# Attention in pairs of steps: one reciprocal a pair, its scaled copy on ScalarE, values and residual one unit later

## The chip, the cores and the metric

The kernel runs on one core of a Trainium2 chip. A core has TensorE (matrix products), VectorE, ScalarE, GpSimd, and SyncE, which here only issues transfers. The engines run side by side and wait for each other through semaphores. The metric is the device time of one execution in microseconds.

## The reference, cut to what matters

Two layers of attention and feed-forward over x of 2 x 256 x 512 with a context of 2 x 512 x 512. The change touches only the softmax attention of the second layer, with 32 query heads, 8 key and value heads and a head width of 128:

```
q, k = rmsnorm(x_norm @ Wq.T), rmsnorm(ctx @ Wk.T)      # 8 key heads serve 4 query heads each
v = ctx @ Wv.T
scores = einsum('bhqd,bhkd->bhqk', q, k) / sqrt(128) + mask
attn   = softmax(scores, axis=-1)
out    = einsum('bhqk,bhkd->bhqd', attn, v)
x      = x + out @ Wo.T
```

After it comes a gated low-rank layer and the store of x.

## The kernel before, in words

All products keep float32 accuracy by splitting each operand into a high half (float16) and a low half (the float16 of what is left): `three_products` (lines 263 to 267) issues three matmuls of 128x128 by 128x512 in place of one.

A **step** is one query head on one tile of 128 tokens against the 512 context positions of its batch: k = 16 g + j, with g one of 8 key heads and j from 0 to 15. Four steps (the four query heads of a key head) on one token tile are a **unit**; there are 32 units and 128 steps. A step goes through the engines like this:

- TensorE: `scores` (line 571), three matmuls into one of four PSUM banks.
- VectorE: `masked_scores` (L1385) adds the mask from SBUF and keeps the row's minimum of the negated scores in `mneg`, writing to one of four slots of `f32r`.
- ScalarE: `exponentials` (L905), with the row sum into `psum_col`.
- VectorE: `inverse_sum` (L1390), the reciprocal of one column, into `rinv[:, 0]`.
- GpSimd: `prob_hi`, first the same reciprocal times 16384 into `rinv[:, 1]` (L1102), then the high half of the probabilities into one of four slots of `hlr` (L1103).
- VectorE: `prob_lo` (L1396), the low half into the same slot, from `f32r`, `rinv[:, 1]` and the high half. It reads two tensors of SBUF.
- SyncE: `prob_transpose` (L353), one DMA transpose of both halves from `hlr` to the unit's buffer `pT[m]`, m the unit's number within g.
- TensorE, per unit: `values` (line 585), 4 x 3 matmuls from `pT` and `v_sb` into bank 4 + m. ScalarE writes the high half of the output (`o_hi`, L910), TensorE subtracts it in the bank (`residual`, L602, one matmul), and ScalarE writes the rest (`o_lo`, L914).

The order on each engine is written out by hand in loops over g, the first of them unrolled. VectorE per step j: scores of j, reciprocal of j - 1, low half of j - 2. TensorE per step: scores of step j (four ahead of VectorE by the banks), at the third step of a unit the residual of the unit before, and a quarter of the values of the unit three back. ScalarE: the exponential, then `o_hi` at the first and `o_lo` at the fourth step of a unit. GpSimd waits for the reciprocal and for the transpose that freed its slot of `hlr` (four steps back). SyncE waits for the low half. After the loops TensorE has the values of the last units and the output projection (`o_group`), a row of products with nothing else among them.

The key lines of VectorE's loop:

```
masked_scores(j, k, m % QT_PER_B, first)
inverse_sum((j - 1) % 4, k - 1)
prob_lo((j - 2) % 4, k - 2, ...)
```

Of the kernel before, what the change touches and what calls it, by code (L numbers as in the profile page):

```python
# [57 lines left out]
def xattn_ffn_kernel(nc, x_rows, ctx_nat, first_chunks, ctx_t, mask, params, wkv, moe, moe_b3, wq, wo, a_w, b_w, l_wq, l_keys, out):  # L58
    gates_dram = nc.dram_tensor("gates_dram", (NE, TOK), F32, kind="Internal").ap()
    with ExitStack() as ctx:  # L60
# [39 lines left out]
        cq = xT[:, :, :, :].rearrange("p a b c -> p (a b c)")  # L100
        xqT = pT1[:, 0:2, :, :].rearrange("p a b (k t) -> p (a b) k t", k=KC)
        ones128 = pT1[:, 2, 0, 0:P]
        pT2 = sb("pT2", [P, 4, 2, GW], F16)
# [122 lines left out]
        s_e = sem("s_e")  # L226
        s_r0 = sem("s_r0")
        s_ph = sem("s_ph")
        s_pl = sem("s_pl")
# [45 lines left out]
        def _(sp):  # L275
# [71 lines left out]

            def prob_transpose(j, split):

                slot = j % 4  # L350
                sp.wait_ge(s_nl, 16 + NT * KVH)
                sp.wait_ge(s_pl, split)
                sp.dma_start_transpose(pT[j // REP][:, slot, :, :].rearrange("p l (c q) -> p (l c) q", c=SC),  # L353
                                       hlr[:, slot, :, :].rearrange("p l x -> p (l x)")).then_inc(s_pT[slot], 16)

            for j in range(4 * REP):
                prob_transpose(j, j + 1)
            with sp.Fori(1, KVH) as g:
                for j in range(4 * REP):
                    prob_transpose(j, sp.to_reg(16 * g + j + 1))  # L360
            for n in range(3, KVH):
# [12 lines left out]
        def _(pe):  # L374
# [209 lines left out]

            def values(w, gw, mw, c, wait_bank=True):

                if c == 0:
                    for h in range(REP):
                        pe.wait_ge(s_pT[h], 16 * (w + 1))
                    if wait_bank:  # L590
                        pe.wait_ge(s_ol, w + 1)
# [12 lines left out]

            def attention(g, first):
                for j in range(4 * REP):
                    k = 16 * g + j
# [29 lines left out]
            for j in range(4):  # L637
                scores(0, j, j, True)
            attention(0, True)
            for h in range(4):  # L640
                pe.wait_ge(s_qT[h], 16 * KVH)
            with pe.Fori(1, KVH) as g:
                attention(g, False)
# [5 lines left out]
            residual(4 * KVH - 2, 2)  # L649
            for c in range(SC):  # L650
                values(4 * KVH - 1, KVH - 1, 3, c)

# [75 lines left out]
        def _(act):  # L728
# [187 lines left out]
            def attention(g, first):  # L916
                for j in range(4 * REP):
                    k = 16 * g + j
                    m, hh = divmod(j, REP)
                    if not first or j >= 3:  # L920
                        exponentials(j, k)
# [7 lines left out]
            for j in range(3):  # L929
                exponentials(j, j)  # L930
            attention(0, True)
            with act.Fori(1, KVH) as g:
                attention(g, False)
            for m in range(2):
                o_hi(4 * KVH - 4 + m, m)
# [76 lines left out]
        def _(pool):  # L1012
# [80 lines left out]

            def prob_hi(j, k, first):
                summed, freed = k + 1, 4 * (k - j)
                if not first:
# [6 lines left out]
                pool.tensor_scalar(hlr[:, j % 4, 0, :], f32r[:, j % 4, :], rinv[:, 0, j % 4:j % 4 + 1], PSCALE,  # L1103
                                   ALU.mult, ALU.mult).then_inc(s_ph, 1)

            for j in range(4):
                prob_hi(j, j, True)
            with pool.Fori(1, 4 * KVH) as u:
                for j in range(4):
                    prob_hi(j, 4 * u + j, False)  # L1110

# [17 lines left out]
        def _(dve):  # L1129
# [257 lines left out]

            def inverse_sum(j, k):
                dve.wait_ge(s_e, k + 1)
                dve.reciprocal(rinv[:, 0, j % 4:j % 4 + 1], psum_col[:, j % 4:j % 4 + 1]).then_inc(s_r0, 1)  # L1390

            def prob_lo(j, k, earlier=None):
# [3 lines left out]
                dve.scalar_tensor_tensor(out=hlr[:, j % 4, 1, :], in0=f32r[:, j % 4, :], scalar=rinv[:, 1, j % 4:j % 4 + 1],  # L1396
                                         in1=hlr[:, j % 4, 0, :], op0=ALU.mult, op1=ALU.subtract).then_inc(s_pl, 1)

            def attention(g, first):
                for j in range(4 * REP):  # L1400
                    k = 16 * g + j
                    m, hh = divmod(j, REP)
                    masked_scores(j, k, m % QT_PER_B, first)
                    if not first or j >= 1:
                        inverse_sum((j - 1) % 4, k - 1)
                    if not first or j >= 2:
                        prob_lo((j - 2) % 4, k - 2, None if first and j < 6 else 4 * g + (j - 2) // REP)

# [3 lines left out]
            end = 16 * KVH  # L1412
            inverse_sum(3, end - 1)
            prob_lo(2, end - 2, 4 * KVH - 1)
            prob_lo(3, end - 1, 4 * KVH - 1)

# [128 lines left out]
```

## Time and profile before

| what | value |
|---|---|
| time, median of 3 runs | 695.01 us (694.28 to 697.63) |
| the profiled execution | 695.37 us, its span 693.2 us |
| busy over the span | TensorE 91%, VectorE 63%, GpSimd 59%, ScalarE 49% |
| attention stage | from about 376 to 574 us |
| after it | output projection on TensorE, to about 640 us, then the last layer |

Times in the rows are microseconds from the start of the span. Busy shares are averages over stages with different limits, so the stage of the change has to be read alone. A wait is put down to the semaphore that came last. PE is TensorE, PEld its weight loads, DVE VectorE, ACT ScalarE, POOL GpSimd, SPq the queue of SyncE.

### The profile page before, as it was taken

What the parts mean: (1) busy time and instruction counts of PE and PEld (TensorE: products, weight loads), DVE (VectorE), ACT (ScalarE), POOL (GpSimd) and SP (SyncE); (2) the same over time, 40 slices, a digit from 0 to 9 for tenths busy, and PEclk for the clock granted to TensorE, in tenths of its full rate; (3) what the DMA queues carried; (4) which work ended last, traced back from release to release, by engine and by line L of the source; (5) the groups of instructions that cost most, each with busy time, mean ns of one, the idle gap of its engine ahead of it and who ended that gap; (6) DMA issues with size and microseconds to landing.
All of it is one profiled execution on the core that took longest, in us unless ns stands there. A gap on an engine that the chain in (4) does not pass through costs nothing.

```text
span 693.2 us, 11377 instructions
## 1 busy us (share of the span) xinstructions
PE 627.6 (91%) x3004; PEld 280.2 (40%) x3004; DVE 438.5 (63%) x1055; ACT 340.1 (49%) x690; POOL 409.8 (59%) x438
## 2 busy tenths in 40 slices
PE   5729989889999999999998779999999999999997
PEld 2314534334444444444443234444444444444453
DVE  5999897253444334755555989999999990000673
ACT  4514544233433332566667566667777663233132
POOL 4923134254455543178787878889898892548111
PEclk9958999899999999999999999999999999999999
DMA  8802034444444432179878999999999995325001
GB/s 327 356 0 76 10 76 99 93 140 148 137 122 136 143 105 96 52 179 180 208 165 221 180 160 172 175 179 175 174 176 174 175 175 106 101 81 183 0 1 61
DMA packets 200312, 95.62 MB, mean 138 GB/s; under 512 B 187962, under 2 KB 188090, under 8 KB 197341
## 3 DMA queue, kind: packets, MB, share of 16 engines
q1 hardware_dynamic: 197490, 90.49, 54.6%
q10 hardware_dynamic: 2795, 4.79, 2.2%
q8 instruction: 14, 0.23, 0.1%
q14 instruction: 13, 0.11, 0.0%
HBM read 48.03 MB, written 1.09 MB: 71 GB/s over the span
## 4 chain that ended last, share of the span: by engine, by line
PE 41%; DVE 19%; issue 16%; POOL 15%; DMA 4%; SPq 2%; ACT 2%; DVEq 1%; POOLq 1%; ACTq 0%
PE ps L265 13%; PE ps L267 13%; PE ps L266 13%; POOL hlr L1103 8%; POOL hlr L1023 4%; POOL wsp L1023 3%; DVE f32r L1385 3%; DVE st L1146 1%; DVE nw L1158 1%; DVE nw L1157 1%; DVE f32r L1162 1%; DMA wsp<-hlr 1%; DMA stage<-in_first_chunks 1%; DVE xT L1221 1%; SPq L314 1%
## 5 line engine op out<-in xcount | busy, mean ns | idle before, releaser
L1023 POOL TENSOR_TENSOR wsp<-stage,wsp 128x512 f16<-128x512 f32 (+1 forms) x93 | 134.5, 1469 | 136.2 <-ACT wsp L761 73.7
L905 ACT ACTIVATE f32r<-f32r,mneg 128x512 f32<-128x512 f32 x128 | 92.4, 722 | 61.1 <-DVE mneg L1385 59.8
L1023 POOL TENSOR_TENSOR hlr<-f32r,hlr 128x512 f16<-128x512 f32 x52 | 60.6, 1173 | 88.3 <-ACT hlr L814 55.0
L1103 POOL TENSOR_SCALAR hlr<-f32r,rinv 128x512 f16<-128x512 f32 x128 | 106.1, 829 | 0.0
L1396 DVE SCALAR_TENSOR_TENSOR hlr<-f32r,rinv,hlr 128x512 f16<-128x512 f32 x128 | 96.0, 750 | 13.0 <-POOL hlr L1103 8.7
L1385 DVE CUSTOM_DVE_ANT_0 f32r<-ps,nmask 128x512 f32<-128x512 f32 x128 | 87.5, 684 | 0.9 <-issue 0.6
L1102 POOL TENSOR_SCALAR rinv<-rinv 128x1 f32<-128x1 f32 x128 | 68.1, 532 | 23.3 <-DVE rinv L1390 11.7
L1354 DVE SCALAR_TENSOR_TENSOR f32r<-ps,par,f32r 128x512 f32<-128x512 f32 x18 | 13.5, 751 | 73.3 <-PE ps L267 60.9
L1304 DVE TENSOR_REDUCE ss<-f32r 128x4 f32<-128x512 f32 x48 | 32.9, 685 | 42.4 <-ACT f32r L802 42.3
L265 PE MATMUL ps<-q_sb 128*128 128x512 f16 x128 | 49.3, 385 | 10.1 <-POOL q_sb L1023 7.3
L265 PE MATMUL ps<-xT,wsp 128*128 128x512 f16 x144 | 55.9, 388 | 2.7 <-DVE stage L1346 2.7
L267 PE MATMUL ps<-xT,wsp 128*128 128x512 f16 x144 | 56.0, 389 | 0.0
L266 PE MATMUL ps<-xT,wsp 128*128 128x512 f16 x144 | 55.9, 389 | 0.0
L265 PE MATMUL ps<-k_sb,q_sb 128*128 (+1 forms) x128 | 49.0, 383 | 7.6 <-DVE mneg L1385 6.2
L265 PE MATMUL ps<-wsp,xT 128*128 128x512 f16 x128 | 48.6, 379 | 2.9 <-POOL wsp L1023 2.8
L802 ACT ACTIVATE f32r<-ps 128x512 f32<-128x512 f32 x48 | 28.6, 597 | 45.1 <-PE ps L267 45.1
L266 PE MATMUL ps<-q_sb 128*128 128x512 f16 x128 | 49.3, 385 | 0.0
L267 PE MATMUL ps<-q_sb 128*128 128x512 f16 x128 | 49.3, 385 | 0.0
L266 PE MATMUL ps<-k_sb,q_sb 128*128 (+1 forms) x128 | 48.8, 381 | 0.0
L267 PE MATMUL ps<-k_sb,q_sb 128*128 (+1 forms) x128 | 48.8, 381 | 0.0
L267 PE MATMUL ps<-wsp,xT 128*128 128x512 f16 x128 | 48.5, 379 | 0.0
L266 PE MATMUL ps<-wsp,xT 128*128 128x512 f16 x128 | 48.5, 379 | 0.0
(229 smaller groups left out, 1298.1 us busy)
## 6 DMA issues: line engine op xcount, KB each, us to landing
stage<-in_moe SPq DMA_DIRECT2D x18, 512.0 KB, 3.8
stage<-in_wq SPq DMA_DIRECT2D x8, 1024.0 KB, 5.2
stage<-in_wo SPq DMA_DIRECT2D x8, 1024.0 KB, 4.8
stage<-in_moe SPq DMA_DIRECT2D x18, 256.0 KB, 3.3
hlr<-gates_dram ACTq DMA_DIRECT2D x18, 256.0 KB, 3.2
k_sb<-in_wkv SPq DMA_DIRECT2D x3, 1024.0 KB, 18.8
stage<-in_first_chunks SPq DMA_DIRECT2D x4, 512.0 KB, 5.8
q_sb<-in_ctx_nat SPq DMA_DIRECT2D x1, 2048.0 KB, 14.9
```

Source lines behind the costliest of these rows:

```text
L265: pe.matmul(dst, lhs[0], rhs[1], start=start, stop=False, skip_group_check=True)
L266: pe.matmul(dst, lhs[1], rhs[0], start=False, stop=False, skip_group_check=True)
L267: return pe.matmul(dst, lhs[0], rhs[0], start=False, stop=stop, skip_group_check=True)
L802: act.activation(f32r[:, j % 2, :], ps[j % 4][:, :], ACT.Square).then_inc(s_sq, 1)
L905: act.activation(f32r[:, j % 4, :], f32r[:, j % 4, :], ACT.Exp, bias=mneg[:, j % 4:j % 4 + 1], scale=-1.0, accum_out=psum_col[:, j % 4:j % ...
L1023: return pool.tensor_tensor(dst_lo, src, dst_hi, ALU.subtract)
L1102: pool.tensor_scalar(rinv[:, 1, j % 4:j % 4 + 1], rinv[:, 0, j % 4:j % 4 + 1], PSCALE, None, ALU.mult)
L1103: pool.tensor_scalar(hlr[:, j % 4, 0, :], f32r[:, j % 4, :], rinv[:, 0, j % 4:j % 4 + 1], PSCALE, ALU.mult, ALU.mult).then_inc(s_ph, 1)
L1304: dve.tensor_reduce(ss[:, j % 2, :], f32r[:, j % 2, :].rearrange("p (h d) -> p h d", h=REP), AX_X, ALU.add).then_inc(s_ss, 1)
L1354: dve.scalar_tensor_tensor(out=tile, in0=bank[:, :], scalar=mb[:, 1, bass.ds(e, 1)], in1=tile, op0=ALU.add, op1=ALU.mult).then_inc(s_hx, 1)
L1385: dve.tensor_tensor_reduce(f32r[:, j % 4, :], ps[j % 4][:, :], nmask[:, qt, :], 0.125, BIG, ALU.add, ALU.min, mneg[:, j % 4:j % 4 + 1]).th ...
L1396: dve.scalar_tensor_tensor(out=hlr[:, j % 4, 1, :], in0=f32r[:, j % 4, :], scalar=rinv[:, 1, j % 4:j % 4 + 1], in1=hlr[:, j % 4, 0, :], op ...
```

## The change: what it does

- VectorE works in pairs of steps. Per pair p: two low halves (of pair p - 2), one reciprocal of two columns (of pair p - 1), two scores (of pair p).
- The scaled copy of the reciprocals (L1102) leaves GpSimd and becomes one ScalarE instruction per pair (`scaled_inverses`), with a new semaphore s_sc that the low halves wait for.
- GpSimd's high half waits for the reciprocal of its pair.
- TensorE computes the values of the unit four back (before: three) and the residual of the unit five back (before: four). After the loop there are three units of values where there were two, ahead of the first and second `o_group`.
- SyncE waits, once per unit, for the values that read the buffer `pT[m]` it is about to overwrite. The low half no longer waits for the transposes itself.

```
+            def halves(j):
+                return hlr[:, j % 4, :, :]
 # SyncE
-            def prob_transpose(j, split):
+            def prob_transpose(j, split, read=None):
                 slot = j % 4
                 sp.wait_ge(s_nl, 16 + NT * KVH)
                 sp.wait_ge(s_pl, split)
+                if read is not None:
+                    sp.wait_ge(s_pv, read)
                 sp.dma_start_transpose(pT[j // REP][...], halves(j)...).then_inc(s_pT[slot], 16)
...
-                    prob_transpose(j, sp.to_reg(16 * g + j + 1))
+                    prob_transpose(j, sp.to_reg(16 * g + j + 1), sp.to_reg(4 * g + j // REP - 3) if j % REP == 0 else None)
 # TensorE
-            def attention(g, first):
+            def attention(g, turn):
                 for j in range(4 * REP):
                     m, c = divmod(j, REP)
-                    if not first or j >= 4:
-                        scores(g, j, k, first)
-                    if c == 2 and not first:
-                        residual(4 * g + m - 4, m)
-                    if not first or m >= 3:
-                        values(4 * g + m - 3, g if m >= 3 else g - 1, (m - 3) % 4, c, not first)
+                    if turn > 0 or j >= 4:
+                        scores(g, j, 16 * g + j, turn == 0)
+                    if c == 2 and (turn > 1 or turn == 1 and m >= 1):
+                        residual(4 * g + m - 5, (m - 1) % 4)
+                    if turn > 0:
+                        values(4 * g + m - 4, g - 1, m, c)
...
-            for w in (1, 2):
+            for w in range(3):
                 for c in range(SC):
-                    values(4 * (KVH - 1) + w, KVH - 1, w, c)
-                residual(4 * (KVH - 1) + w - 1, w - 1)
+                    values(tail_unit + w, KVH - 1, w, c)
+                residual(tail_unit + w - 1, (w - 1) % 4)
 # ScalarE
+            def scaled_inverses(j, pair):
+                act.wait_ge(s_r0, pair + 1)
+                act.activation(rinv[:, 1, j:j + 2], rinv[:, 0, j:j + 2], ACT.Copy, scale=PSCALE).then_inc(s_sc, 1)
...
+                    if j % 2 == 0 and (not first or j >= 2):
+                        scaled_inverses((j - 2) % 4, 8 * g + j // 2 - 1)
+                    exponentials(j, k)
 # GpSimd
-                summed, freed = k + 1, 4 * (k - j)
+                summed, freed = 2 * u + j // 2 + 1, 16 * u
...
-                pool.tensor_scalar(rinv[:, 1, j % 4:j % 4 + 1], rinv[:, 0, j % 4:j % 4 + 1], PSCALE, None, ALU.mult)
 # VectorE
+            def inverse_sums(j, pair):
+                dve.wait_ge(s_e, 2 * pair + 2)
+                dve.reciprocal(rinv[:, 0, j:j + 2], psum_col[:, j:j + 2]).then_inc(s_r0, 1)
+            def prob_lo(j, k, pair):
+                dve.wait_ge(s_sc, pair + 1)
                 dve.wait_ge(s_ph, k + 1)
-                if earlier is not None:
-                    dve.wait_ge(s_pT[j % 4], 16 * earlier)
...
             def attention(g, first):
+                for p in range(2 * REP):
+                    a, pair = 2 * p, 8 * g + p
+                    if not first or p >= 2:
+                        for j in range(2):
+                            prob_lo((a - 4 + j) % 16, 16 * g + a - 4 + j, pair - 2)
+                    if not first or p >= 1:
+                        inverse_sums((a - 2) % 4, pair - 1)
+                    for j in (a, a + 1):
+                        masked_scores(j, 16 * g + j, j // REP % QT_PER_B, first)
```

## Rows read from the trace of the kernel before

**Rows 1.** The page, part 1: busy time, share of the span, instructions.
```profile
PE 627.6 (91%) x3004; PEld 280.2 (40%) x3004; DVE 438.5 (63%) x1055; ACT 340.1 (49%) x690; POOL 409.8 (59%) x438
```
**Rows 2.** Windows: length, busy PE, PEld, DVE, ACT, POOL, then PEclk, DMA share, GB/s.
```profile
396.00:568.00 172.00, 156.97 (x698) 67.96 (x698) 160.45 (x456) 119.03 (x284) 152.20 (x228) 0.99 0.92 174
...
572.00:590.00 18.00, 18.00 (x85) 8.14 (x84) 1.10 (x3) 6.97 (x15) 5.58 (x6) 1.00 0.48 101
```
**Rows 3.** Waits from 400 to 568: who for whom, total us, times, longest.
```profile
PEld ps L602 <- issue: 28.4, 28, 4.1
PE ps L602 <- ACT q_sb L910: 14.8, 26, 3.6
...
DVE f32r L1385 <- PE ps L267: 0.3, 1, 0.3
```
**Rows 4.** By line: instructions, duration in ns (min/median/max), first and last start in us.
```profile
L905 ACT ACTIVATE f32r<-f32r,mneg x128: 706/722/725, 378.6 to 569.5; 128x512 f32<-128x512 f32 x128
...
L1396 DVE SCALAR_TENSOR_TENSOR hlr<-f32r,rinv,hlr x128: 731/750/753, 380.7 to 572.4; 128x512 f16<-128x512 f32 x128
...
L1102 POOL TENSOR_SCALAR rinv<-rinv x128: 204/582/755, 379.8 to 570.9; 128x1 f32<-128x1 f32 x128
...
L1103 POOL TENSOR_SCALAR hlr<-f32r,rinv x128: 688/691/1197, 380.0 to 571.1; 128x512 f16<-128x512 f32 x128
```
**Rows 5.** Timeline in the loop, VectorE and GpSimd: start, duration, what.
```profile
450.56 0.69 POOL L1103 TENSOR_SCALAR hlr<-f32r,rinv 128x512 f16<-128x512 f32 x1
...
451.35 0.21 POOL L1102 TENSOR_SCALAR rinv<-rinv 128x1 f32<-128x1 f32 x1
451.39 0.75 DVE L1396 SCALAR_TENSOR_TENSOR hlr<-f32r,rinv,hlr 128x512 f16<-128x512 f32 x1 [0.20 <-POOL hlr L1103]
451.53 1.18 POOL L1103 TENSOR_SCALAR hlr<-f32r,rinv 128x512 f16<-128x512 f32 x1
...
452.06 0.69 DVE L1385 CUSTOM_DVE_ANT_0 f32r<-ps,nmask 128x512 f32<-128x512 f32 x1
...
452.75 0.75 DVE L1396 SCALAR_TENSOR_TENSOR hlr<-f32r,rinv,hlr 128x512 f16<-128x512 f32 x1
```
**Rows 6.** Timeline at the start of the kernel, VectorE and GpSimd.
```profile
20.75 4.13 POOL L1038 TENSOR_SCALAR q_sb<-q_sb,par 128x2048 f32<-128x2048 f32 x2
...
21.01 1.82 DVE L1159 SCALAR_TENSOR_TENSOR nw<-nw 128x4 f32<-128x4 f32 x1
```
**Rows 7.** Timeline at the head of the attention, VectorE and GpSimd.
```profile
376.52 0.68 DVE L1385 CUSTOM_DVE_ANT_0 f32r<-ps,nmask 128x512 f32<-128x512 f32 x1
...
377.13 0.69 DVE L1385 CUSTOM_DVE_ANT_0 f32r<-ps,nmask 128x512 f32<-128x512 f32 x1
...
379.42 0.17 DVE L1390 RECIPROCAL rinv<-psum_col 128x1 f32<-128x1 f32 x1 [1.60 <-ACT f32r L905]
379.57 0.69 DVE L1385 CUSTOM_DVE_ANT_0 f32r<-ps,nmask 128x512 f32<-128x512 f32 x1
379.75 0.23 POOL L1102 TENSOR_SCALAR rinv<-rinv 128x1 f32<-128x1 f32 x1 [1.26 <-DVE rinv L1390]
```
**Rows 8.** SyncE's transposes: timeline in the loop, and landing of all of them.
```profile
452.23 1.23 SPq L353 DMA_TRANSPOSE pT<-hlr  x1
...
453.63 1.24 SPq L353 DMA_TRANSPOSE pT<-hlr  x1
...
DMA to landing us min/median/max: 3.1/3.3/4.8
```
**Rows 9.** By line, ScalarE: duration in ns (min/median/max), first and last start in us.
```profile
L808 ACT ACTIVATE root<-ss,par x48: 283/288/298, 80.4 to 374.6; 128x4 f32<-128x4 f32 x48
...
L910 ACT ACTIVATE q_sb<-ps x32: 575/577/597, 402.4 to 587.8; 128x512 f32 x28, 128x512 f16<-128x512 f32 x4
```
**Rows 10.** Timeline of TensorE behind the loop, the values of one unit.
```profile
571.61 0.38 PE L265 MATMUL ps<-pT,v_sb 128*128 128x512 f16 x1
...
574.20 0.38 PE L602 MATMUL ps<-q_sb,negid 128*128 128x512 f16 x1
```

More of the change, by code:

```diff
@@ L227, in xattn_ffn_kernel @@
         s_r0 = sem("s_r0")
+        s_sc = sem("s_sc")
         s_ph = sem("s_ph")
@@ L352, in prob_transpose @@
                 sp.wait_ge(s_pl, split)
+                if read is not None:
+                    sp.wait_ge(s_pv, read)
                 sp.dma_start_transpose(pT[j // REP][:, slot, :, :].rearrange("p l (c q) -> p (l c) q", c=SC),
-                                       hlr[:, slot, :, :].rearrange("p l x -> p (l x)")).then_inc(s_pT[slot], 16)
+                                       halves(j).rearrange("p l x -> p (l x)")).then_inc(s_pT[slot], 16)
             for j in range(4 * REP):
@@ L583, in scores, with values @@
                     [k_sb[:, bass.ds(g, 1), l, b * CTX:(b + 1) * CTX] for l in range(2)], True, True).then_inc(s_s, 1)
-            def values(w, gw, mw, c, wait_bank=True):
+            def values(w, gw, mw, c):
                 if c == 0:
@@ L589, in values @@
                         pe.wait_ge(s_pT[h], 16 * (w + 1))
-                    if wait_bank:
-                        pe.wait_ge(s_ol, w + 1)
+                    pe.wait_ge(s_ol, w + 1)
                 last = three_products(
@@ L638, in _ @@
                 scores(0, j, j, True)
-            attention(0, True)
+            attention(0, 0)
             for h in range(4):
                 pe.wait_ge(s_qT[h], 16 * KVH)
-            with pe.Fori(1, KVH) as g:
-                attention(g, False)
-            for w in (1, 2):
+            attention(1, 1)
+            with pe.Fori(2, KVH) as g:
+                attention(g, 2)
+            tail_unit = 4 * (KVH - 1)
+            for w in range(3):
                 for c in range(SC):
-                    values(4 * (KVH - 1) + w, KVH - 1, w, c)
-                residual(4 * (KVH - 1) + w - 1, w - 1)
+                    values(tail_unit + w, KVH - 1, w, c)
+                residual(tail_unit + w - 1, (w - 1) % 4)
             o_group(0, 0, True)
-            residual(4 * KVH - 2, 2)
+            residual(tail_unit + 2, 2)
             for c in range(SC):
-                values(4 * KVH - 1, KVH - 1, 3, c)
+                values(tail_unit + 3, KVH - 1, 3, c)
             o_group(1, 1, False)
@@ L919, in attention @@
                     m, hh = divmod(j, REP)
-                    if not first or j >= 3:
-                        exponentials(j, k)
+                    if j % 2 == 0 and (not first or j >= 2):
+                        scaled_inverses((j - 2) % 4, 8 * g + j // 2 - 1)
+                    exponentials(j, k)
                     if hh == 0 and not first:
@@ L928, in _ @@
             rms_phase(16, 4, 2 * NT, 1.0 / 64, scs[:, 13:14], s_qT, 16, q_quarter)
-            for j in range(3):
-                exponentials(j, j)
             attention(0, True)
@@ L933, in _ @@
                 attention(g, False)
+            scaled_inverses(2, 8 * KVH - 1)
             for m in range(2):
@@ L1091, in _, with prob_hi @@
             rms_phase(16, 4, 2 * NT, lambda i, s, c: quarter_lo(1 - s, c, 8 * i + 4 + 4 * s + c))
-            def prob_hi(j, k, first):
-                summed, freed = k + 1, 4 * (k - j)
+            def prob_hi(j, u, first):
+                summed, freed = 2 * u + j // 2 + 1, 16 * u
                 if not first:
@@ L1101, in prob_hi @@
                     pool.wait_ge(s_pT[j], freed)
-                pool.tensor_scalar(rinv[:, 1, j % 4:j % 4 + 1], rinv[:, 0, j % 4:j % 4 + 1], PSCALE, None, ALU.mult)
-                pool.tensor_scalar(hlr[:, j % 4, 0, :], f32r[:, j % 4, :], rinv[:, 0, j % 4:j % 4 + 1], PSCALE,
+                pool.tensor_scalar(halves(j)[:, 0, :], f32r[:, j, :], rinv[:, 0, j:j + 1], PSCALE,
                                    ALU.mult, ALU.mult).then_inc(s_ph, 1)
             for j in range(4):
-                prob_hi(j, j, True)
+                prob_hi(j, 0, True)
             with pool.Fori(1, 4 * KVH) as u:
                 for j in range(4):
-                    prob_hi(j, 4 * u + j, False)
+                    prob_hi(j, u, False)
             for c in range(4):
@@ L1386, in masked_scores @@
                                          ALU.add, ALU.min, mneg[:, j % 4:j % 4 + 1]).then_inc(s_t, 1)
[L1388 to L1392, printed above, removed]
+            def inverse_sums(j, pair):
[3 more added lines that the diff above has]
+                dve.wait_ge(s_sc, pair + 1)
                 dve.wait_ge(s_ph, k + 1)
-                if earlier is not None:
-                    dve.wait_ge(s_pT[j % 4], 16 * earlier)
-                dve.scalar_tensor_tensor(out=hlr[:, j % 4, 1, :], in0=f32r[:, j % 4, :], scalar=rinv[:, 1, j % 4:j % 4 + 1],
-                                         in1=hlr[:, j % 4, 0, :], op0=ALU.mult, op1=ALU.subtract).then_inc(s_pl, 1)
+                dve.scalar_tensor_tensor(out=halves(j)[:, 1, :], in0=f32r[:, j % 4, :], scalar=rinv[:, 1, j % 4:j % 4 + 1],
+                                         in1=halves(j)[:, 0, :], op0=ALU.mult, op1=ALU.subtract).then_inc(s_pl, 1)
             def attention(g, first):
[L1400 to L1407, printed above, removed]
+                for p in range(2 * REP):
[7 more added lines that the diff above has]
+                        masked_scores(j, 16 * g + j, j // REP % QT_PER_B, first)
             attention(0, True)
@@ L1412, in _ @@
             end = 16 * KVH
-            inverse_sum(3, end - 1)
-            prob_lo(2, end - 2, 4 * KVH - 1)
-            prob_lo(3, end - 1, 4 * KVH - 1)
+            for j in range(2):
+                prob_lo(12 + j, end - 4 + j, 8 * KVH - 2)
+            inverse_sums(2, 8 * KVH - 1)
+            for j in range(2):
+                prob_lo(14 + j, end - 2 + j, 8 * KVH - 1)
             dve.wait_ge(s_lw, 2)
```

1 line of the change is left out of this document (removed).

## The prediction

> **What bounds the kernel now.** I read the shares by engine first, then the stage of the change alone, then the waits in it, and last the instructions one by one, because the bound is a hand-over that no share shows. Over the span TensorE is busy 91% [rows 1], but the attention stage has its own limit: from 396 to 568 us TensorE works 157.0 of 172.0 us, VectorE 160.5, GpSimd 152.2, and the DMA engines 92% of the time [rows 2]. Four resources stand close to full, so the waits decide. TensorE loses time once per unit of four steps at the residual product (28 "issue" waits, 28.4 us, of which 14.8 us on ScalarE's copy), yet VectorE waited for TensorE 0.3 us in all [rows 3]. That idle time is slack of TensorE and not the bound.
>
> The bound is the pair VectorE and GpSimd. Per step GpSimd writes the high half (L1103, 0.69 us) and VectorE the low half (L1396, 0.75 us) [rows 4]. In [rows 5] one low half starts at 451.39; the high half of the next step, issued at 451.53, takes 1.18 instead of 0.69 us, so it really began at 452.71 - 0.69 = 452.02, 0.63 after the start of the low half. It ends at 452.71 and its own low half starts at 452.75. The two kinds never run together. GpSimd is held by VectorE's instruction with two SBUF operands. The other direction is seen too: GpSimd's TENSOR_SCALAR x2 from 20.75 (2.06 each) holds a tiny VectorE instruction of the same kind for 1.82 us, until 22.83 [rows 6]. A VectorE instruction of a few columns takes about 0.17 [rows 7], so it got going at 22.66, 0.15 before the end of GpSimd's first at 22.81. The scores instruction (L1385) blocks nothing: the high half at 450.56 runs its normal 0.69.
>
> So today a step is one high and one low half in turn. The first high half starts at 380.0 and the last at 571.1 [rows 4]: 191.1 us for 127 steps, 1.505 a step, **3.01 us per two steps**. In that cycle the small scaling on GpSimd (L1102, 0.58 when it meets a low half) mostly waits for the same hand-over [rows 4, 5].
>
> **The change, part by part.** Call the effective start of the first low half of a pair 0.
> - Low halves: the second starts when VectorE goes on, 0.67 after the first (451.39 to 452.06 [rows 5]); the reciprocal is then issued at 1.34.
> - Reciprocal: one for two columns. For one column the row has 0.17, and the next instruction starts 0.15 after it (379.42, 379.57) [rows 7]. For two columns I take 0.16; the outside case is twice the row, 0.34, which would add 0.17 per pair. It ends at 1.50. GpSimd starts 0.16 later (379.42 + 0.17 to 379.75 [rows 7]), at 1.66. **This is the new cost:** before, the reciprocal of a step ran while GpSimd was held anyway; now both high halves of the pair wait for a reciprocal that stands behind both low halves.
> - High halves: 1.66 to 2.35, then 0.10 to the next instruction (451.25 to 451.35 [rows 5]), so the second runs from 2.45 to 3.14.
> - Scores, two: at 1.49 and 2.10 (0.61 apart, 376.52 to 377.13 [rows 7]). From a scores instruction to the low half behind it are 0.69 (452.06 to 452.75 [rows 5]), so VectorE is free for the next low half at 2.79.
> - Next low half: its data has been ready since 2.35, but the second high half holds it. If GpSimd lets go 0.15 before its end, as in [rows 6], it starts at 2.99; if only at the end plus 0.04, as a dependent low half does, at 3.18. The first is a measured release, so I take the lower part, **3.05 per pair by the hand-over alone**.
> - Scaled copy on ScalarE: nearest rows are an ACTIVATE of 128x4, 0.29 us [rows 9], and one of 128x512, 0.72 [rows 4]. From 1.50 + 0.16 it is done by 1.95, or 2.4 at worst; the low half wants it at 3.0. ScalarE would be waiting for the scores at that time. I cost it at nothing; without that cover it would be 0.3 per pair.
> - L1102 removed: worth the gap between a release at +0.63 and a high half at +0.79 (0.16 per step) only if the high half were ready at the release. Now it isn't, it waits for the reciprocal, so this gain is replaced by the line above.
>
> SyncE and the four slots of hlr: a transpose starts 0.09 to 0.13 after its low half (452.14 to 452.23, 453.50 to 453.63) and the next 1.40 after it [rows 8]. With the low halves 0.67 apart, the first transpose starts at 0.86 and the second at 2.26. It lands 3.3 later (median) [rows 8], at 5.56, and only then, plus 0.16, may GpSimd write that slot again, 5.72. In the following pair that write is due at T + 2.45. The cycle closes at T = (5.72 + 0.60) / 2 = **3.16**, with 0.60 from a high half's start to the next low half. Landings are given as 3.1 at least, which makes it 3.06. The new ring has two pairs of room where the old one had four steps one by one, and the second transpose of a pair loses 0.7 us queued behind the first. New wait on s_pv before the first transpose of a unit: those values are issued on TensorE at least four steps before; SyncE, with every later transpose and, through them, GpSimd behind it, would pay, but I see no lateness and take 0 to 0.05 per pair.
>
> I take **T = 3.12**, close to the ring, since the larger of two limits counts. 63 pairs x (3.12 - 3.01) = **+6.9 us**.
>
> Head: the first reciprocal now waits for two exponentials instead of one, one more of 0.72 [rows 4]: **+0.7 us**.
>
> Values and residual one unit later: in the loop this takes away the residual waits of TensorE, which as shown nobody feels. ScalarE's high copy of the output now waits for values that end only just before; worked from the scores before them it has some 0.7 us of slack. At the end, one more unit of values stands behind the last scores, 12 matmuls, where TensorE is busy 18.00 of 18.00 us [rows 2]. Twelve of them and nothing else stretch from 571.61 to 574.20, 0.216 each [rows 10], so 2.6 us, and one more residual, 0.2: **+2.8 us**. Its lower bound is 2.0, if a wait before the first residual of the tail goes.
>
> Sum: 6.9 + 0.7 + 2.8 = +10.4. The profiled execution took 695.4 us (span 693.2), 0.4 above the median of 695.0, so I leave that out: **705.8 us**.
>
> The Trainium skill, page "SBUF — State Buffer", section "A bandwidth-pool intuition that's wrong (but worth ruling out)", gives a later hand-over than the rows: the loser goes on about 115 ns after the holder's end. [Rows 5] say 0.12 before it (452.02 against 452.14). That figure belongs to descriptor writing by GpSimd, so I follow the row; by the page T would be 3.14 + 0.115 = 3.25 and the sum about 714, an estimate of mine from its figure.
>
> **Rivals.**
> (a) Forecast, T between 3.02 and 3.2: 700 to 711.
> (b) The other side: a high half does not hold the low half of the other step (no row shows a 128x512 low half held by a high half; [rows 6] show it only for a small one), or lets go so early that it never matters. Then VectorE's own 2.79, SyncE's 2 x 1.40 = 2.80, and the ring without the hold, (5.72 + 0.73 - 0.67) / 2 = 2.89, remain. ScalarE comes in as well: with an output copy (0.58 [rows 9]) between the two exponentials of 0.72, the second one's sum is ready at about 4.4, while the reciprocal is due at T + 1.34, so every other pair costs about 3.1. The mean lies between 2.89 and 3.0: 63 x (-0.12) + 3.5 = -4.1, 691.3, to 63 x (-0.01) + 3.5, 698. With SyncE alone as the limit it is 63 x (-0.21) + 3.5 = -9.7, 685.7. It decides below T = 2.95, where the loop gives back more than the head and the tail cost. For it: GpSimd loses an instruction per step, and it is the resource of the cycle. Against: [rows 5, 6].
> (c) Order slips: a landing over 3.4 us moves the second high half past 2.79, the low half goes first and the high half waits behind it. A pair of 2.79 is then followed by one of 3.7, mean 3.26: 63 x 0.25 + 3.5 = +19, 714.7, up to 720 if ScalarE's output copy is also late for its values. For: landings reach 4.8 [rows 8]. Against: the median is 3.3, and the slower loop relieves the DMA engines.
> (d) The change does what it says for TensorE and that is worth it: its 28.4 us of waits would be the price. I give this nothing of its own; the 0.3 us of VectorE waiting for it [rows 3] exclude it.
>
> **Numbers.** (a) 0.55, (b) 0.30, (c) 0.15. What a measurement can tell from no change is 0.5%, about 3.5 us. Faster: 0.17, the lower half of (b). Within: 0.18, the rest of (b) and the lowest edge of (a). Slower: 0.65. The likeliest case has 700 to 711 for itself; for 8 in 10 the range is 688 to 716.
>
> **What would show it.** Timeline of a unit: low, low, reciprocal, then two high halves beside two scores, and the next low half lasting 0.9 to 1.2 instead of 0.75, since it is issued into a running high half; a pair of 3.1. TensorE's waits at the residual gone, and new waits at the scores' product (for VectorE) in their place. SyncE's transposes 1.40 and 1.7 apart. Wrong: low halves all at 0.75 beside running high halves, a pair of 2.9 or less, or GpSimd waiting mostly on DMA.

## The result, and the profile after

The changed kernel takes 699.11 us (median of 8 runs, 698.29 to 701.16) against 695.61 us; the ratio is 1.0052, 95% interval 1.0036 to 1.0068. It is slower, as forecast, but by 3.5 us and not by 10.4. The profiled execution took 698.95 us with a span of 697.2, 4.0 more than before, and I account for those 4.0.

The busy times barely move for TensorE and fall for GpSimd, which has lost 128 instructions. The page, part 1, of the changed kernel:

```profile
PE 634.1 (91%) x3004; PEld 281.2 (40%) x3004; DVE 435.6 (62%) x991; ACT 346.0 (50%) x754; POOL 335.7 (48%) x310
```

Against [rows 1] GpSimd went from 409.8 to 335.7 us and the kernel got slower: its busy time was no measure of the bound. The waits from 400 to 570 us in the changed kernel (who for whom, total, times, longest) say what it does instead:

```profile
POOL hlr L1113 <- DVE rinv L1400: 72.2, 55, 1.5
PEld ps L270 <- issue: 35.5, 58, 1.8
...
DVE hlr L1405 <- POOL hlr L1113: 14.9, 21, 1.4
PE ps L270 <- DVE mneg L1395: 13.2, 32, 1.3
...
POOL hlr L1113 <- DMA wsp<-hlr: 6.6, 9, 1.8
POOL hlr L1113 <- DMA pT<-hlr: 5.2, 11, 0.6
POOL hlr L1113 <- DMA xT<-hlr: 2.8, 4, 0.9
```

The residual waits of [rows 3] are gone from TensorE. It now waits for VectorE's scores. The three DMA rows are the important ones: 24 waits for a transpose, 14.6 us in all, and 21 low halves that then wait for the high half. By line (ns min/median/max, first and last start), and the landing of all transposes:

```profile
L1113 POOL TENSOR_SCALAR hlr<-f32r,rinv x128: 688/694/1249, 381.1 to 575.5; 128x512 f16<-128x512 f32 x128
...
L1405 DVE SCALAR_TENSOR_TENSOR hlr<-f32r,rinv,hlr x128: 736/750/1156, 382.1 to 576.6; 128x512 f16<-128x512 f32 x128
...
L1400 DVE RECIPROCAL rinv<-psum_col x64: 149/158/167, 380.7 to 574.5; 128x2 f32<-128x2 f32 x64
...
L917 ACT ACTIVATE rinv<-rinv x64: 203/203/205, 380.9 to 574.7; 128x2 f32<-128x2 f32 x64
...
DMA to landing us min/median/max: 3.0/3.3/5.0
```

The longest low half went from 753 ns [rows 4] to 1156: low halves are now issued into running high halves and held. The 64 reciprocals start from 380.75 to 574.49, which is 3.075 us per pair. The single periods are not near that mean: 36 of the 63 are 2.79 to 2.84 (mean 2.81), and 27 are long (mean 3.43), in most of the loop two short ones and a long one. Three of the long ones take 3.9 to 4.1; in each of them a high half waits 1.5 to 1.8 us for a transpose. A short pair in the timeline:

```profile
452.62 0.16 DVE L1400 RECIPROCAL rinv<-psum_col 128x2 f32<-128x2 f32 x1
452.70 0.67 DVE L1395 CUSTOM_DVE_ANT_0 f32r<-ps,nmask 128x512 f32<-128x512 f32 x1
...
452.94 1.36 POOL L1113 TENSOR_SCALAR hlr<-f32r,rinv 128x512 f16<-128x512 f32 x2 [1.02 <-DVE rinv L1400]
...
453.90 1.59 DVE L1405 SCALAR_TENSOR_TENSOR hlr<-f32r,rinv,hlr 128x512 f16<-128x512 f32 x2
...
454.13 0.58 ACT L921 ACTIVATE q_sb<-ps 128x512 f32 x1
...
454.61 0.71 ACT L912 ACTIVATE f32r<-f32r,mneg 128x512 f32<-128x512 f32 x1
...
455.22 0.19 ACT L912 ACTIVATION_READ_ACCUMULATOR f32r<-f32r,mneg 128x1 f32 x1
...
455.44 0.17 DVE L1400 RECIPROCAL rinv<-psum_col 128x2 f32<-128x2 f32 x1
```

From the reciprocal 0.32 to the first high half, 0.67 to the second (453.61), which runs to 454.30. The two low halves are issued at 453.90 and take 1.59, where two that aren't held take 1.42 (the pair at 456.91), so the first was held for 0.17 and began at 454.07, 0.46 after the second high half began. Then 1.37 to the next reciprocal: 0.32 + 0.67 + 0.46 + 1.37 = 2.82. A second chain ends at the same moment here: ScalarE has an output copy (0.58) between its two exponentials, so the second row sum is ready at 455.41 (455.22 + 0.19), 0.03 before the reciprocal. So ScalarE may set this pair as well. The long pair just before it:

```profile
450.61 0.75 DVE L1405 SCALAR_TENSOR_TENSOR hlr<-f32r,rinv,hlr 128x512 f16<-128x512 f32 x1
...
450.72 1.20 POOL L1113 TENSOR_SCALAR hlr<-f32r,rinv 128x512 f16<-128x512 f32 x1 [0.55 <-DMA pT<-hlr]
...
451.95 0.75 DVE L1405 SCALAR_TENSOR_TENSOR hlr<-f32r,rinv,hlr 128x512 f16<-128x512 f32 x1 [0.59 <-POOL hlr L1113]
```

The second high half waits for the transpose that frees its slot, and a low half gets in first. The high half then takes 1.20 behind it, and the second low half waits for that. This pair costs 3.47.

**Where the 4.0 us are.** I cut the stage at four instructions: VectorE's first scores (step 0), its scores of step 123, TensorE's products of step 127 (which need the bank of step 123) and the first product of the output projection. The last three, in the kernel before and then in the changed one:

```profile
562.82 0.68 DVE L1385 CUSTOM_DVE_ANT_0 f32r<-ps,nmask 128x512 f32<-128x512 f32 x1
...
567.20 0.38 PE L265 MATMUL ps<-k_sb,q_sb 128*128 x1
...
574.41 0.38 PE L265 MATMUL ps<-wsp,q_sb 128*128 128x512 f16 x1
```
```profile
566.25 0.69 DVE L1395 CUSTOM_DVE_ANT_0 f32r<-ps,nmask 128x512 f32<-128x512 f32 x1
...
568.00 0.38 PE L270 MATMUL ps<-k_sb,q_sb 128*128 x1
...
578.45 0.38 PE L270 MATMUL ps<-wsp,q_sb 128*128 128x512 f16 x1
```

| us | before | changed | difference |
|---|---|---|---|
| start of the stage (376.52, 377.14) | | | +0.6 |
| loop on VectorE, step 0 to 123 | 186.3 | 189.1 | +2.8 |
| lag: TensorE behind VectorE at the end | 4.4 | 1.75 | -2.6 |
| tail, products of 127 to projection | 7.2 | 10.45 | +3.2 |

The start is not the change's: it lay between 375.3 and 379.1 in the profiles of this study.

### The profile page after: what moved, and what is told of

Read it like the earlier page. It is cut to its first block, busy times and chain, and to the rows that moved or that the text cites. A ratio compares the mean times of both kernels' runs of the same rounds, so it can differ in the third digit from the quotient of the medians.

```text
span 697.2 us, 11213 instructions
## 1 busy us (share of the span) xinstructions
PE 634.1 (91%) x3004; PEld 281.2 (40%) x3004; DVE 435.6 (62%) x991; ACT 346.0 (50%) x754; POOL 335.7 (48%) x310
## 4 chain that ended last, share of the span: by engine, by line
PE 45%; DVE 20%; issue 10%; DMA 9%; POOL 9%; SPq 4%; ACT 2%; DVEq 1%; POOLq 0%; ACTq 0%
PE ps L270 15%; PE ps L272 15%; PE ps L271 15%; SPq L360 4%; POOL wsp L1034 3%; POOL hlr L1034 3%; DMA pT<-hlr 3%; DMA wsp<-hlr 3%; DMA xT<-hlr 3%; DVE hlr L1405 2%; POOL hlr L1113 2%; DVE st L1156 1%; DVE nw L1168 1%; DVE nw L1167 1%; DVE f32r L1172 1%
## 5 line engine op out<-in xcount | busy, mean ns | idle before, releaser
L1113 POOL TENSOR_SCALAR hlr<-f32r,rinv 128x512 f16<-128x512 f32 x128 | 96.6, 762 | 100.4 <-DVE rinv L1400 83.5
L1405 DVE SCALAR_TENSOR_TENSOR hlr<-f32r,rinv,hlr 128x512 f16<-128x512 f32 x128 | 98.5, 794 | 18.5 <-POOL hlr L1113 18.4
L1395 DVE CUSTOM_DVE_ANT_0 f32r<-ps,nmask 128x512 f32<-128x512 f32 x128 | 82.3, 679 | 1.2
L270 PE MATMUL ps<-k_sb,q_sb 128*128 (+1 forms) x128 | 50.1, 391 | 22.5 <-DVE mneg L1395 20.3
L270 PE MATMUL ps<-q_sb 128*128 128x512 f16 x128 | 50.5, 395 | 10.1 <-POOL q_sb L1034 7.3
L272 PE MATMUL ps<-q_sb 128*128 128x512 f16 x128 | 50.2, 392 | 0.0
L271 PE MATMUL ps<-q_sb 128*128 128x512 f16 x128 | 50.2, 392 | 0.0
L272 PE MATMUL ps<-k_sb,q_sb 128*128 (+1 forms) x128 | 49.6, 388 | 0.0
L271 PE MATMUL ps<-k_sb,q_sb 128*128 (+1 forms) x128 | 49.6, 387 | 0.0
L893 ACT CAST wsp<-stage 128x512 f16<-128x512 f32 x56 | 31.2, 616 | 24.4 <-PE ps L272 24.4
```

Source lines behind the costliest of these rows:

```text
L270: pe.matmul(dst, lhs[0], rhs[1], start=start, stop=False, skip_group_check=True)
L271: pe.matmul(dst, lhs[1], rhs[0], start=False, stop=False, skip_group_check=True)
L272: return pe.matmul(dst, lhs[0], rhs[0], start=False, stop=stop, skip_group_check=True)
L893: act.copy(wsp[:, slot, 0, c * GW:(c + 1) * GW], stage[:, slot, c * GW:(c + 1) * GW]).then_inc(s_wqh, 1)
L1113: pool.tensor_scalar(halves(j)[:, 0, :], f32r[:, j, :], rinv[:, 0, j:j + 1], PSCALE, ALU.mult, ALU.mult).then_inc(s_ph, 1)
L1395: dve.tensor_tensor_reduce(f32r[:, j % 4, :], ps[j % 4][:, :], nmask[:, qt, :], 0.125, BIG, ALU.add, ALU.min, mneg[:, j % 4:j % 4 + 1]).th ...
```

## Experiments

All times are medians, ratios against runs of the kernel before on the same chip, with 95% intervals.

### TensorE's part alone

```
 # kernel before, TensorE
-    values(4 * g + m - 3, ...)      residual(4 * g + m - 4, m)      for w in (1, 2):
+    values(4 * g + m - 4, ...)      residual(4 * g + m - 5, ...)    for w in range(3):
 # SyncE, once a unit
+    sp.wait_ge(s_pv, read)
```

> The kernel before with only TensorE's part of the change: values four units back, residual five back, three units of values behind the loop, and SyncE's wait on s_pv. Theory (my prediction's sum counted the end twice): the residual waits of TensorE cost nothing inside the loop (3.01 us per two steps stays), but they leave TensorE 3.7 us behind VectorE at the loop's end (scores 127 start at 567.2, their bank is free from 563.5; in the changed kernel 1.1 us). Without them that lag shrinks to about 1 us, and one more unit of values (2.8) comes behind: -2.6 + 2.8, so 695.3 to 696.5 against 695.6 of before. Rival 1 (the prediction's term as it stood): the lag is worth nothing, the full +2.8, 698.4. Rival 2: the residual waits were felt in the loop, the period falls under 2.95 and the kernel is faster than 692.

Measured: 695.92 us against 695.8, ratio 1.0002 (0.9988 to 1.0015). The same three instructions:

```profile
565.53 0.68 DVE L1387 CUSTOM_DVE_ANT_0 f32r<-ps,nmask 128x512 f32<-128x512 f32 x1
...
566.36 0.39 PE L265 MATMUL ps<-k_sb,q_sb 128*128 x1
...
577.11 0.38 PE L265 MATMUL ps<-wsp,q_sb 128*128 128x512 f16 x1
```

Loop 186.7 (first scores at 378.87), lag 0.8, tail 10.75: against before +0.4, -3.55, +3.55. Inside the loop the residual waits cost next to nothing, as predicted. At its end they did cost something: they kept TensorE more than 4 us behind. What I charged to the longer tail was paid back by a shorter lag.

### The pairs without TensorE's part

```
 # changed kernel, TensorE: the old order
-    values(4 * g + m - 4, ...)      residual(4 * g + m - 5, ...)    for w in range(3):
+    values(4 * g + m - 3, ...)      residual(4 * g + m - 4, m)      for w in (1, 2):
```

> The changed kernel with TensorE's old order: values three units back, residual four back, two units of values behind the loop; pairs, reciprocal and scaled copy as changed. Theory: the pair period stays at 3.075 us; the extra unit behind the loop goes (-2.8 to -3.3), TensorE's lag at the loop's end comes back (+2.6): 698 to 699.2 against 699.1 of the changed kernel. Rival 1: the lag is worth nothing, 696. Rival 2: in pairs TensorE has too little room for the residual waits (2.67 us of products in a pair of 2.81), VectorE then waits for scores, the period rises to 3.15 or more, 702 to 705.

Measured: 701.67 us, 1.0083 (1.0068 to 1.0099), 2.5 us slower than the changed kernel. The mean pair is 3.10 and the pattern one short, one long (2.81 and 3.38). Its waits from 400 to 560 us:

```profile
PEld ps L609 <- issue: 31.1, 25, 3.3
...
PE ps L609 <- ACT q_sb L921: 18.8, 25, 2.8
...
DVE f32r L1395 <- issue: 6.9, 24, 0.3
```

Two instructions around one of those 24 waits:

```profile
469.78 0.38 PE L272 MATMUL ps<-k_sb,q_sb 128*128 x1
...
470.29 0.69 DVE L1395 CUSTOM_DVE_ANT_0 f32r<-ps,nmask 128x512 f32<-128x512 f32 x1 [0.28 <-issue]
```

The scores start 0.13 after TensorE's last product for them ends (470.16), so it is TensorE that they wait for. Loop 190.7, lag 5.3, tail 7.1, against 189.1, 1.75 and 10.45 in the changed kernel: the end is the same and the loop is 1.6 longer.

Neither theory as written. My estimate of 698 to 699.2 was too low. The second rival has the right kind (VectorE is stopped ahead of its scores 24 times, by 0.3 us) at a third of its size. So TensorE's part is worth nothing in single steps and about 2.5 us in pairs.

### The scaled copy alone, in single steps

```
 # kernel before, GpSimd
-    pool.tensor_scalar(rinv[:, 1, ...], rinv[:, 0, ...], PSCALE, None, ALU.mult)
 # ScalarE, behind each exponential, for the step before
+    act.wait_ge(s_r0, k + 1)
+    act.activation(rinv[:, 1, j:j + 1], rinv[:, 0, j:j + 1], ACT.Copy, scale=PSCALE).then_inc(s_sc, 1)
 # VectorE, ahead of each low half
+    dve.wait_ge(s_sc, k + 1)
...
```

> The kernel before with only the scaled copy of the reciprocal moved to ScalarE, one instruction per step (128 of 0.2 us); single steps, TensorE's order untouched. Theory: in single steps the high half is ready when the low half lets go, so without L1102 it starts at +0.63 instead of +0.79 in most steps: hi + 0.73, lo + 0.63, 1.36 to 1.40 per step, where SyncE's 1.40 per transpose limits; two steps 2.80 to 2.86 against 3.01. 63 x (-0.15 to -0.21) = -9.5 to -13: 682.5 to 686. Rival 1: four slots of hlr and the landing of 3.3 us hold the ring, the period stays at 2.95 to 3.01: 692 to 695.6. Rival 2: the added 0.2 us on ScalarE comes between an exponential and the next and delays the row sums: no gain or slower, 695 to 698.

Measured: 690.25 us, 0.9913 (0.9892 to 0.9934). Half of the theory's gain. The hand-over in the timeline:

```profile
470.91 0.75 DVE L1401 SCALAR_TENSOR_TENSOR hlr<-f32r,rinv,hlr 128x512 f16<-128x512 f32 x1
471.00 1.23 POOL L1107 TENSOR_SCALAR hlr<-f32r,rinv 128x512 f16<-128x512 f32 x1 [0.28 <-DVE rinv L1394]
...
472.31 0.75 DVE L1401 SCALAR_TENSOR_TENSOR hlr<-f32r,rinv,hlr 128x512 f16<-128x512 f32 x1
```

The high half ends at 472.23, so it began at 471.54, 0.63 after the low half, and the step is 1.40. But one or three such steps are followed by one of 1.51 to 1.53, and from 400 to 550 us 20 high halves wait for a transpose.

### All of the change but the pairs

The two edits above together, on the kernel before.

> All of the change but the pairs: single steps, scaled copy on ScalarE per step, values and residual one unit later, four slots. It gives the pairs' own share at four slots. Theory: the parts add up. TensorE's order was worth 0 (lag -3.6, tail +3.5), the scaled copy -5.5: 689 to 691, so the pairs alone cost 8 to 10 us against 699.1. Steps of 1.40 with 1.52 mixed in as before. Rival: the pairs only cost because TensorE's order goes with them; then this one is no faster than 694.

Measured: 689.92 us, 0.9908 (0.9891 to 0.9925). Loop 180.6, lag 0.85, tail 10.65, so the parts add up (differences of medians, each good to 1 to 1.5 us): 0 for TensorE's order, -5.5 for the scaled copy, and **about +9 us for the pairs** at four slots. The loss comes from the pairs alone.

### Eight slots for the halves, in pairs and in single steps

```
 # changed kernel; slots 4 to 7 in the stage buffer, its load of wo[2] after the last transpose
     def halves(j):
-        return hlr[:, j % 4, :, :]
+        if j % 8 < 4: return hlr[:, j % 4, :, :]
+        return stage[:, 0, :].bitcast(F16).rearrange("p (s l c) -> p s l c", s=4, l=2)[:, j % 4, :, :]
```

> The changed kernel with eight slots for the halves instead of four (four in hlr, four in the stage buffer whose next weight load is issued after the last transpose), and eight transpose semaphores. Theory: the changed kernel's mean pair of 3.075 us is two of 2.82 and one of 3.47, and the long one is a second high half that waits for the transpose of its slot and lets a low half go first. With eight slots the long pairs vanish, the period is 2.80 to 2.86 (SyncE 2 x 1.40, low, low, reciprocal, high, high 2.82): 63 x (-0.22 to -0.27) = -14 to -17, 682 to 685. Rival 1: the DMA engines are the limit (92% busy at 2.99 us per two steps, so 2.75 at 100%): landings grow, the period ends between 2.9 and 3.0, 688 to 694. Rival 2: the long pairs come from ScalarE's output copies in every second pair: period unchanged, 699.

Measured: 688.47 us, 0.9896 (0.9881 to 0.9912). All 63 pairs take 2.79 to 2.82. The ring was the cause of the long ones, and ScalarE's output copies were not. The sum came out smaller, since the end grew. Busy from 420 to 550 us (PE, PEld, DVE, ACT, POOL, then clock, DMA share, GB/s), and TensorE's waits from 550 to 600:

```profile
420.00:550.00 130.00, 128.98 (x580) 56.41 (x580) 128.41 (x324) 102.04 (x278) 62.70 (x92) 1.00 0.98 182
```
```profile
PE ps L272 <- DMA xT<-stage: 2.1, 1, 2.1
PE ps L272 <- DMA pT<-hlr: 1.1, 1, 1.1
```

The compute ran ahead of the transposes (1.44 apart in the mean, mostly 1.40 to 1.43 with one of 1.7 in 16, against 1.405 per step), and TensorE waited for the last ones. Behind the wait of 2.1 us its granted clock was 0.50 (1.2 GHz) from 559.3 to 562.6, and its products took 0.63 each instead of 0.38. Lag and tail together are 16.6 against 12.2 in the changed kernel. The same eight slots in single steps, with the scaled copy on ScalarE:

> The kernel before with the scaled copy on ScalarE (as in the run before) and eight slots for the halves (four in hlr, four in the stage buffer, its next weight load issued after the last transpose); single steps, TensorE's old order. Without pairs the second transpose of a pair does not queue, and 1.40 a step was met with 1.52 mixed in at four slots (mean 1.464 from the first scores to those of step 123). Theory: the 1.52 are waits of the ring; with eight slots all steps take 1.40, the limit is SyncE: loop 172.6 instead of 180.8, end of the loop some 4 us longer since the transposes lag, 685 to 687. Rival 1: the 1.52 come from ScalarE, which has 0.2 us more per step and two output copies per unit: unchanged, 690. Rival 2: the DMA engines are already at the limit: steps of 1.44, 689.

Measured: 687.17 us, 0.9883 (0.9856 to 0.991); from the 26th step on all are 1.40 to 1.43, no more 1.52, and no high half waits for a transpose. Pairs (2.81 for two steps) and single steps (2.82) have the same period once the ring is long enough. Early in the loop two steps took 2.75 and 2.52, and there a residual wait of TensorE (this version has the old order) was felt after all:

```profile
403.42 0.61 PE L610 MATMUL ps<-q_sb,negid 128*128 x1 [3.44 <-ACT q_sb L922]
...
406.72 0.69 DVE L1396 CUSTOM_DVE_ANT_0 f32r<-ps,nmask 128x512 f32<-128x512 f32 x1 [1.25 <-PE ps L273]
...
409.24 0.69 DVE L1396 CUSTOM_DVE_ANT_0 f32r<-ps,nmask 128x512 f32<-128x512 f32 x1 [1.09 <-issue]
```

TensorE idled 3.44 us, its granted clock was then 0.50 from 403.4 to 408.9 (products of 0.63), and VectorE had to wait for its scores. The kernel before has the same once, after an idle stretch of 3.57 at 403.09, and it costs VectorE 0.28 and 0.59.

### Transposes of half the bytes, four slots

This version leaves the low halves out of the values: only the high halves are transposed, and the products read them twice, so that the number of products stays.

```
 # changed kernel
-    sp.dma_start_transpose(pT[j // REP][:, slot, :, :]..., halves(j)...)
+    sp.dma_start_transpose(pT[j // REP][:, slot, 0, :]..., halves(j)[:, 0, :])
 # TensorE, values: the halves that the products read
-    [pT[mw][:, :, l, c * P:(c + 1) * P] for l in range(2)]
+    [pT[mw][:, :, 0, c * P:(c + 1) * P] for l in range(2)]
```

> The changed kernel with four slots, where each transpose moves the high half only (128 x 512, half the bytes) and the products of values read it in place of the low one too: the low halves' part of the values is left out, the number of matmuls stays. Theory (ring): the landing falls under 2.7 us and the issue to 0.6 to 0.7, so no high half waits for its slot; the long pairs vanish with four slots as they did with eight: all pairs at 2.81 or less (VectorE and GpSimd alone), and the end of the loop is not longer: 63 x -0.26 = -16.6, 681 to 683. If VectorE and GpSimd alone can do less than 2.81 (SyncE's 2 x 1.40 being the true limit), 678 to 681. Rival: the long pairs remain because they come from ScalarE's output copies or the s_pv wait: 695 to 699.

Measured: 684.25 us, 0.984 (0.982 to 0.9859). SyncE's row and the landing:

```profile
L360 SPq DMA_TRANSPOSE pT<-hlr x64: 1188/1189/1219, 393.5 to 562.9; - x64
...
DMA to landing us min/median/max: 2.4/2.4/4.4
```

With the landing at 2.4 instead of 3.3 us, 61 of 63 pairs are 2.79 to 2.83 with the old four slots; the other two (3.7 and 4.3) still wait for a transpose. The issue time hardly moved (1.19 against 1.25), against my 0.6 to 0.7, so the landing did it. With the DMA engines at 46% the pair still takes 2.81. I had worked 2.82 out of the chain of VectorE and GpSimd, but SyncE's two issues stayed near 1.4 each here, so the two are not told apart by this run; the next one takes SyncE out.

### One transpose per pair

```
 # SyncE
-    sp.dma_start_transpose(pT[...][:, slot, :, :]..., halves(j)...).then_inc(s_pT[...], 16)
+    sp.dma_start_transpose(pT[...][:, slot:slot + 2, :, :]..., ring[:, slot:slot + 2, :, :]...).then_inc(...)   # every second j
```

With eight slots (TensorE and GpSimd then wait for the transpose of the pair):

> The changed kernel with eight slots and one DMA transpose per pair of steps (128 x 2048) instead of two of 128 x 1024; the same bytes. It separates SyncE's issue from the DMA engines. Theory A: SyncE's 1.23 us is per instruction, and it is the limit of the eight-slot version (transposes 1.44 apart, the last 5 us behind its low half): the lag at the end goes, 684 to 686. Theory B: the issue time grows with the bytes (2.4 us for the double one) or the DMA engines, 99% busy in that version, are the limit: 688 to 690, the end as long as before, and a landing of 4 us or more. The pair period stays 2.81 in both.

Measured: **683.11 us, 0.982 (0.9798 to 0.9841)**, the fastest version. SyncE's rows and the landing:

```profile
L363 SPq DMA_TRANSPOSE wsp<-hlr x16: 1878/2005/3101, 384.0 to 544.0; - x16
...
L363 SPq DMA_TRANSPOSE pT<-stage x16: 1451/1643/1972, 400.8 to 560.9; - x16
...
DMA to landing us min/median/max: 4.2/4.5/6.1
```

SyncE is mostly busy 1.5 to 2.0 us of each 2.81 and the pair is 2.81 still, so neither SyncE nor the ring sets it. What is left is the chain of VectorE and GpSimd, but not it alone: in every second pair the reciprocal starts 0.03 us after ScalarE's second row sum, which stands behind an output copy. The two chains agree to some 0.03 us, and no run here tells them apart. The last transpose is issued at 560.9 instead of 567.0, and TensorE waits for no transpose behind the loop. Theory A holds for the time (684 to 686 expected, a little more gained), though the issue does grow with the bytes. With the four slots of the changed kernel:

> The changed kernel with its four slots and one transpose per pair (128 x 2048). It tests the ring's formula at another landing: 4.2 to 4.5 us instead of 3.3. The transpose starts at 1.37 + 0.75 + 0.1 = about 1.5 after the lead of the pair (second low half at 0.67 to 1.42), lands at 5.7 to 6.0, plus 0.13, then two high halves and the next low half 0.67 + 0.46 later, which closes after two periods: T = (5.85 to 6.15 + 1.13) / 2 = 3.49 to 3.64 for every pair. Against 3.08 of the changed kernel that is 63 x (0.41 to 0.56) = +26 to +35: 725 to 734. Rival: the long pairs are SyncE's issue (2 x 1.40 against 2.0 for the double one); then this one has none, 683 to 688.

Measured: 732.67 us, 1.0526 (1.0502 to 1.055); landing 4.2 us, pairs of 3.0 and 4.05 in turn, mean 3.60. The formula of the ring gave 3.49 to 3.64 and 725 to 734. It gives the mean also where it is spread over unequal pairs. The rival, by which the long pairs were SyncE's issue, would have had 683 to 688.

### The reciprocal ahead of the low halves

```
 # VectorE, per pair
+    inverse_sums(...)
     prob_lo(...); prob_lo(...)
-    inverse_sums(...)
```

> The changed kernel with the pair's reciprocal ahead of the two low halves instead of behind them. My prediction named its place behind them as the new cost (0.32 us between the second low half and the first high half). Theory: that place is forced: ahead of them it waits for the exponentials of the scores just made. Cycle: reciprocal 0.08, low halves 1.34, first scores 0.61, then 0.12, two exponentials 0.73 + 0.63, sum 0.19: 3.7 us a pair or more, 63 x 0.6 = +38, 730 to 745. Rival: the exponentials are early enough, the high halves start 0.3 us sooner, long pairs become rarer, 692 to 697.

Measured: 778.0 us, 1.1199 (1.117 to 1.1228); pairs of 4.12 and 4.6. The place behind the low halves is forced, by more than I worked out (3.7 a pair, 730 to 745 us); I did not pursue the rest of the cycle, and its cause stays open.

## Why the prediction was right or wrong

- **Mechanism: right in kind.** Hand-over between low and high halves both ways (low halves up to 1156 ns), TensorE's residual waits gone with no gain in the loop (first experiment: loop 186.7 against 186.3), scaled copy hidden (no low half waits for it; 0.203 us), head (380.75 - 377.14 against 379.42 - 376.52, +0.7).
- **Ring of four slots: right as a mean.** I had 3.06 to 3.16 for it and 3.075 was measured. That the order would slip was my rival (c). It isn't a rival: it is how the ring's limit shows, two pairs of 2.81 and one of about 3.4. (Its own mean, of 2.79 and 3.7, is 3.25 and not 3.26.) The formula with the median landing gives 3.16; with the hold of 0.46 in place of 0.60 it gives (5.72 + 0.46) / 2 = 3.09.
- **First step that failed, the hand-over: mis-sized.** The step "3.05 per pair by the hand-over alone" measured 2.82 at most (ScalarE's chain ends with it). Two terms of it were long: high half to high half 0.67 instead of 0.79 (I took the gap before the small scaling, an instruction that is no longer there), and GpSimd let go 0.46 after its start instead of 0.54 to 0.73. So the hand-over didn't bind, and T = 3.12, put "close to the ring", was 0.045 too high: 63 x 0.045 = 2.8 us of the miss.
- **Second step that failed: "the residual waits of TensorE, which as shown nobody feels", with "+2.8 us" at the end.** In the loop they are hardly felt: my 0.3 us left out one wait of 0.59 us behind a slow stretch of TensorE, as shown above, and without all residual waits the loop was no shorter. At its end they had left TensorE 4.4 us behind VectorE, and from there to the projection TensorE's work is the time. The change removes 2.6 us of that lag, which cancels most of the longer tail (3.2); alone, without the pairs, it cancels all of it (-3.55, +3.55). I had put at most 0.8 on this.
- Those two make 5.4 of the 6.9 us between +10.4 and +3.5. The rest, 1.5 us, is a net sum that I read from the two traces and did not test. From the first to the last high half the changed kernel takes 3.3 more (381.1 to 575.5 against 380.0 to 571.1) and not 63 x 0.065 = 4.1, because the last one follows the first of its pair by 0.67 instead of a whole step of 1.5. And the scores of step 123, on which TensorE's last products wait, stand 9.2 ahead of the last high half instead of 8.3, as the second of their pair. Those are 1.7 us that my sum, counted by the high halves, did not see; the head, taken up to the first high half, grew by 0.5 (3.95 against 3.43) and not 0.7, which adds 0.2; a tail 0.4 longer goes against them, and so do the 0.6 of the later start, while the medians lie 0.5 closer together than the profiled executions. (My 705.8 also stands on the profiled 695.4; from the median it would be 705.4.)
- Of the removed small scaling I wrote that its gain "is replaced by the line above". The third experiment shows what was there: 5.5 us in single steps. The pairs gave that away and 3.5 more, most of it by the ring of four slots, as the versions with eight slots and with half the bytes show.
- By the later hand-over of the Trainium skill (page "SBUF — State Buffer", section "A bandwidth-pool intuition that's wrong (but worth ruling out)") the sum would have been about 714 by my estimate. The runs do not agree: a low half let go 0.12 before its recorded end, as in [rows 5], and a high half 0.23 before it.

## What to carry to other kernels

A ring of buffers limits the period by the latency around it, and grouping steps shortens the ring: pairs in four slots are a ring of two. Work it out as latency over slots before grouping, and lengthen the ring (or use the grouping for one transfer per group) in the same change. Idle time of an engine off the critical path can still be a debt that falls due where the loop ends and that engine's own queue becomes the time. So compare the lag there, not only the waits.

## What the runs showed of the hardware

- Transposes from SBUF to SBUF, per 128 partitions, by their width: 512 columns took SyncE 1.19 us and landed after 2.4, 1024 columns 1.25 and 3.3, 2048 columns 1.6 to 2.0 (medians by group) and 4.2 to 4.5. Issue and landing grow far slower than the bytes, so one double transfer beat two with eight slots (683.1 against 688.5 us) and lost with four (732.7 against 699.1).
- The DMA engines showed 98% to 100% busy (182 to 188 GB/s) from 420 to 550 us in the two eight-slot versions in pairs, and the pair was 2.81 us, as with 46% in the version with half the bytes. The full share alone was no limit.
- A GpSimd high half (0.69 us) let a waiting low half start 0.46 after its own start, 0.23 before its recorded end. A low half (0.75) let a high half go on 0.63 after its own start (the scaled copy alone, and [rows 5]).
- After an idle stretch of TensorE of 3.57 us (kernel before) and of 3.44 (single steps, eight slots) the granted clock was 0.50, the level of 1.2 GHz, for 3.3 and 5.5 us, and a product of 128x512 took 0.63 instead of 0.38. Not every idle stretch had this behind it: 2.21 us before 381.6 had in the changed kernel, and 2.21 before 380.9 had not in the version with half the bytes.
